# The end of an attention layer, and the start of the refinement behind a mixture of experts, arranged anew

## The reference, cut to what matters

```python
x = x + layernorm(attention(layernorm(x)))        # x: (8, 1024, 256), 16 heads of 16 + 8 dims
x = x + layernorm(ffn(layernorm(x)))

def ffn(x):                                        # 8192 rows of 256
    xf, v, integrated = x, 0, x
    idx, weight = top2(softmax(gelu(xf @ router_w1 + router_b1) @ router_w2 + router_b2))
    for _ in range(2):
        ctx = concat(integrated, v)
        shared = gelu(ctx @ shared_w1 + shared_b1) @ shared_w2 + shared_b2
        chosen = [gelu(ctx @ w1[e] + b1[e]) @ w2[e] + b2[e] for e in idx]
        # sigmoid, softplus and sigmoid of the thirds of each give a step against (x - mu);
        # the three steps are mixed, and a halting gate scales the mix
        integrated, v = ...
    refined = gelu(integrated @ refine_w1 + refine_b1) @ refine_w2 + refine_b2
    return xf + integration_weight * refined
```

## Time and profile before

| | |
|---|---|
| Median of three runs | 2930.03 us (2920.26 to 2935.52) |
| The profiled execution's own time | 2933.28 us |
| Its span | 2931.6 us |
| PE, DVE, ACT, POOL busy, share of the span | 88%, 77%, 66%, 21% |
| Mean granted TensorE clock | 0.936 of full speed |

### The profile page before, as it was taken

One profiled execution on the slowest core, in us unless ns is written; L12 is line 12 of the kernel. 1 busy time (PEld: TensorE's weight loads), 2 busy tenths in 40 slices (PEclk: granted clock), 3 DMA queues, 4 the chain that ended last, 5 costly groups with the idle time before them and its releaser, 6 DMA issues. The chain is left out here.

```text
span 2931.6 us, 43059 instructions
## 1 busy us (share of the span) xinstructions
PE 2591.9 (88%) x16032; PEld 1799.7 (61%) x16032; DVE 2269.5 (77%) x3931; ACT 1933.7 (66%) x3075; POOL 608.6 (21%) x424
## 2 busy tenths in 40 slices
PE   3788888888888967899999999999999999997997
PEld 2233333333323313688888888788788888886897
DVE  4577777667676656789889998999989988886555
ACT  1676766667676844566667666666767766665786
POOL 2012031211112111111121121211111121210476
PEclk8899989999898967899999999999999999999999
DMA  3552525254351631000000000000000000000442
GB/s 101 87 86 61 91 65 92 75 90 79 67 101 52 93 90 51 1 1 15 15 1 15 15 15 8 8 16 15 15 1 15 15 15 8 1 8 27 147 133 73
DMA packets 125634, 136.75 MB, mean 47 GB/s; under 512 B 17410, under 2 KB 105474, under 8 KB 125428
## 3 DMA queue, kind: packets, MB, share of 16 engines
q1 hardware_dynamic: 125428, 134.00, 20.1%
HBM read 87.56 MB, written 46.40 MB: 46 GB/s over the span
## 5 line engine op out<-in xcount | busy, mean ns | idle before, releaser
L491 ACT ACTIVATE probs<-psum_a 128x1024 f32<-128x1024 f32 (+3 forms) x768 | 601.1, 815 | 333.9 <-PE psum_a L807 329.6
L1487 PE MATMUL psum_f<-w,picked 128*128 128x256 f32 (+1 forms) x2304 | 712.3, 342 | 0.0
L1486 PE MATMUL psum_f<-w,picked 128*128 128x256 f32 x2304 | 617.4, 285 | 1.2 <-DVE picked L1306 1.2
L1487 PEld LDWEIGHTS psum_f<-w,picked 128*128 128x128 f32 x2304 | 444.5, 193 | 51.5
L567 DVE TENSOR_SCALAR probs<-probs 128x2048 f32<-128x2048 f32 (+3 forms) x320 | 304.0, 950 | 203.6 <-ACT probs L491 203.6
L807 PE MATMUL psum_a<-q_stack,k_stack 72*128 72x512 f16 (+3 forms) x1536 | 396.3, 349 | 56.3 <-ACT probs L491 35.0
L1486 PEld LDWEIGHTS psum_f<-w,picked 128*128 128x128 f32 x2304 | 445.1, 193 | 1.5 <-DVE picked L1306 1.5
L822 PE MATMUL psum_a<-probs,v 128*17 128x512 f32 (+3 forms) x3072 | 342.8, 520 | 10.6 <-DVE attn L579 5.9
L807 PEld LDWEIGHTS psum_a<-q_stack,k_stack 72*128 72x128 f16 x1536 | 100.6, 101 | 400.8 <-ACT probs L491 238.7
L1306 DVE TENSOR_TENSOR picked<-hid,masks 128x512 fp32r<-128x512 f32 x512 | 335.0, 714 | 10.0 <-PE psum_f L1487 6.8
L1127 ACT ACTIVATE gates<-psum_f 128x256 f32<-128x256 f32 (+1 forms) x384 | 186.4, 487 | 233.1 <-PE psum_f L1487 231.3
(11 more groups left out here) (289 smaller groups left out, 5408.2 us busy)
## 6 DMA issues: line engine op xcount, KB each, us to landing
heads_scratch<-kq_parts SPq DMA_DIRECT2D x64, 256.0 KB
k_stack<-heads_scratch SPq DMA_DIRECT2D x96, 128.0 KB
q_stack<-heads_scratch SPq DMA_DIRECT2D x96, 128.0 KB
x_in<-x_dram SPq DMA_DIRECT2D x8, 1024.0 KB, 5.5
x_res<-x_dram SPq DMA_DIRECT2D x16, 512.0 KB, 4.8
x_scratch<-y SPq DMA_DIRECT2D x16, 512.0 KB, 3.1
xs<-x_scratch SPq DMA_DIRECT2D x16, 512.0 KB, 3.9
xf_scratch<-xs SPq DMA_DIRECT2D x16, 512.0 KB, 2.9
```

The costliest lines, as they stand in the source:

```text
L491: act.activation(probs[:, s % PROB_SETS, 2 * u:2 * u + 2, q0:512], psum[:, 2 * u:2 * u + 2, q0:512], ACT.Exp, scale=exp_scale).then_inc(ex ...
L1486: pe.matmul(soft_out, x, cols[:, 1], start=start, stop=stop)
L1487: return pe.matmul(gate_out, x, cols[:, 2] if it == 0 else cols[:, 0::2], start=start, stop=stop)
```

## The change

- SP's order in window 7: the residual and the store of batch 6's first half now stand ahead of the 56 weight loads, which have moved from the end of window 6 to there. Behind them SP waits until V of batch 6 is no longer read, and loads the first 512 rows of x1 (`x_first`) over it.
- The ten split steps move from ticks 360 to 369 to ticks 373 to 382. In ticks 372 to 377 PE multiplies the unsplit weights by mu (`mean_column`, 12 matmuls), and DVE corrects the biases (job "MU").
- At tick 383 DVE takes the statistics of `x_first`, POOL the power, and at tick 386 DVE normalizes it, subtracted from mu. The mixture's PE starts with XT at once.
- The last half of batch 7 has a buffer of its own, `y_last`, so ACT's copy doesn't wait for the store. Block 1 of the mixture's rows lies over `y_last`, so its load waits until all stores have landed.
- DVE's constants (`first_values`) come behind the lower parts of block 0's transposes, not ahead of its statistics.
- Refinement's weights are loaded over the first layer's when block 15's last hidden job is done; DVE splits them in steps behind `integrate` of units 124 to 127; PE multiplies them by mu behind its last unit; the first two blocks of xf are loaded over `hid`. SP no longer waits for the last stores of xf at the end of the mixture; two loads of xf in the refinement do.

```diff
     for t, (kind, half, i) in OUTPUT.items(): ...
+    MEAN_TICK = (BATCH - 1) * STEPS + 36
+    MEAN_COLS = 6
+    job_at[MEAN_TICK + MEAN_COLS - 1] = ("MU", BATCH - 1, 0, 0)
+    SPLIT_TICK = MEAN_TICK + 1
+    X_FIRST_TICK = ALL_STEPS - 1
...
             for w in range(-1, BATCH + 1):   # SP, attention
                     load_residual(before, 0)
                     store_rows(before, 0)
                     load_residual(before, 1)
+                if w == BATCH - 1:
+                    sp.wait_ge(late_cleared, 1)
+                    for dst, src in late_loads:
+                        sp.dma_start(dst, src).then_inc(late_in, 16)
+                    sp.wait_ge(pv_done, STEPS * w)
+                    sp.dma_start(late.x_first[:], ...[0]).then_inc(x_first_in, 16)
...
-                if after == BATCH - 1:
-                    sp.wait_ge(late_cleared, 1)
-                    for dst, src in late_loads:
-                        sp.dma_start(dst, src).then_inc(late_in, 16)
...
                 if kind == "OR":
-                    if (b, half) != (0, 0):
+                    if (b, half) == (BATCH - 1, 1):
+                        act.wait_ge(pv_done, STEPS * b)
+                    elif (b, half) != (0, 0):
                         act.wait_ge(x1_stored, 16 * (2 * b + half))
-                    dst = y[:, 2 * i:2 * i + 2, :]
+                    dst = y_of(b, half)[:, 2 * i:2 * i + 2, :]
...
-                if w == BATCH - 1 and 24 <= t < 24 + late.SPLITS:
-                    split_late(t - 24)
+                if tick == X_FIRST_TICK:
+                    first_stats()
+                if tick == X_FIRST_TICK + 3:
+                    first_normalize()
+                if SPLIT_TICK <= tick < SPLIT_TICK + late.SPLITS:
+                    split_late(tick - SPLIT_TICK)
...
+            def mean_column(m):          # PE, attention
+                if m == 0:
+                    pe.wait_ge(late_in, 16 * len(late_loads))
+                    bank_free(job)
+                for c in range(2):
+                    last = pe.matmul(bank[0:w.shape[1], m:m + 1], w, late.mu_col[:, c:c + 1], ...)
...
         def _(sp):                       # mixture
-            sp.wait_ge(late.x1_stored, 16 * XS)
-            for k in range(XS):
+            for k in (2, 3, 1):
+                if k == 1:
+                    sp.wait_ge(late.x1_stored, 16 * BLOCKS)
                 sp.dma_start(xs[:, k], blk_v[k]).then_inc(x_loaded[k], 16)
-            sp.wait_ge(late.x1_stored, 16 * BLOCKS)
             for k in range(BLOCKS):
+                if k == BLOCKS - 1:
+                    job_ready(sp, ("H", k, 1, FULL - 1))
+                    for dst, src in refine_loads:
+                        sp.dma_start(dst, src).then_inc(late.f_in, 16)
+                    sp.wait_ge(upper_picked, 2 * n + 2)
+                    sp.wait_ge(lower_picked, 2 * n + 2)
+                    for q in range(2):
+                        sp.dma_start(late.xf[:, q], xf_v[q]).then_inc(late.xf_loaded[q], 16)
                 sp.wait_ge(unit_done, first_unit[k, 1] + BT)
...
-            for q in range(XS):
-                sp.wait_ge(xf_stored[q], 16 * len(range(q, BLOCKS, XS)))
...
-            x_row_stats(0)
-            first_values()
-            x_normalize(0)
             for c in range(2):
                 x_lower(0, 0, c)
+            first_values()
             x_row_stats(1)
...
+                if n >= UNITS - BT:
+                    split_refine(t)
...
-            for m in range(6):           # PE, mixture: 24 matmuls by mu, then the wait
-                ...
-            pe.wait_ge(weights_ready, 1)
...
+            pe.wait_ge(late.f_split, 2)  # PE, behind the last unit: 16 matmuls by mu
...
-            for dst, src in loads:       # SP, refinement
-                sp.dma_start(dst, src).then_inc(weights_in, 16)
             for k in range(AHEAD):
-                load_xf(k)
+                if k >= 2:
+                    load_xf(k)
                 load_x1(k)
```

More of the change, by code:

```diff
@@ L226, in attention, with y_of @@
         half_neg = sb("half_neg", [P, TILES])
+        def y_of(b, half):
+            return late.y_last if (b, half) == (BATCH - 1, 1) else y
         heads_dram = nc.dram_tensor("heads_scratch", (2, 2, 2, 2 * P, SEQ), F16, kind="Internal").ap()
@@ L1404, in _ @@
             pe.wait_ge(late.split, late.SPLITS)
-            for m in range(6):
-                for c in range(2):
-                    for part in range(2):
-                        w = w1[:, part, c, P * m:P * m + P] if m < 5 else wr1[:, part, c]
-                        last = pe.matmul(psum[0:w.shape[1], 0, m:m + 1], w.bitcast(F32), mu_col[:, c:c + 1],
-                                         start=(c == 0 and part == 0), stop=(c == 1 and part == 1))
-            last.then_inc(mu_part, 1)
-            pe.wait_ge(weights_ready, 1)
             def bank_free(job):
@@ L1517, in _, with refine @@
                     run(item)
-def refine(nc, late, x1_dram, consts_dram, w_dram, xf_dram, row_scale, out_dram):
+            for job in jobs[-3:]:
+                bank_read(pe, job)
+            pe.wait_ge(late.f_split, 2)
+            for m in range(MC):
+                for c in range(2):
+                    for part in range(2):
+                        last = pe.matmul(psum[:, 0, m:m + 1], late.wf1[:, part, c, P * m:P * m + P].bitcast(F32), mu_col[:, c:c + 1],
+                                         start=(c == 0 and part == 0), stop=(c == 1 and part == 1))
+            last.then_inc(late.f_mean, 1)
+def refine(nc, late, x1_dram, xf_dram, out_dram):
     x1_v = x1_dram.rearrange("(i t p) d -> i p t d", p=P, t=BT)
@@ L1525, in refine @@
     BLOCKS = TOKENS // BLOCK
-    mean, rstd = row_scale[:, 0], row_scale[:, 1]
+    mean, rstd = late.row_scale[:, 0], late.row_scale[:, 1]
     BUFS, AHEAD = 6, 4
@@ L1783, in _ @@
         def _(pe):
-            pe.wait_ge(weights_in, 16 * len(loads))
-            for m in range(MC):
-                for c in range(2):
-                    last = pe.matmul(psum[:, 0, m:m + 1], raw_f1[:, c, P * m:P * m + P], mu_col[:, c:c + 1], start=(c == 0), stop=(c == 1))
-            last.then_inc(mu_part, 1)
-            pe.wait_ge(weights_ready, 1)
+            pe.wait_ge(late.f_split, 4)
             for job in order:
@@ L1877 @@
         attention(nc, late, x, consts, attn_w, ffn_w, x1)
-        feed_forward(nc, late, x1, consts, ffn_w, xf, out)
+        mixture(nc, late, x1, ffn_w, xf)
+        refine(nc, late, x1, xf, out)
     r = run(nc, [arrays], core_ids=[0])
```

212 lines of the change are left out of this document (134 added, 78 removed).

## The result

The changed kernel takes 2899.39 us (median of 7 runs, 2894.30 to 2907.54) against 2930.03 (7 runs, 2920.26 to 2935.52). The ratio is 0.990, 95% interval 0.988 to 0.992: faster by 30.6 us, where 47 were forecast. 2899 lies in the range of 2868 to 2906. The places where instructions were moved gave 45.6 us in the profile, of the 46.7 that were summed for them. Part of the gain was lost again at a place where no instruction was changed: between its first and its last store the mixture took 14.2 us more. The prediction had named this as a sign of being wrong (over 3 us more or less between the mixture's first lower part and its last store): it was 1521.0 us (1183.46 to 2704.41) and is 1535.5 (1150.58 to 2686.05). So the time came out inside the range, and one step of the reasoning did not hold.

A forecast was written before the change was run, and what follows sets the result against it. The prediction took PE to bound the mixture, PE, DVE and ACT to share the attention, and PE to wait at both program borders. Its terms summed to -46.7 us, 2886.6 profiled, a median of 2883, range 2868 to 2906.

The forecast's parts named there:

- The stall: Window 7: ACT's wait for the store of `y`, behind the 56 loads, goes whole, -19.0 us; half clock behind it, -2.7.
- The rival of a moved stall: Window 7: ACT still waits for a store, or PE for late loads at tick 372; 2904 us, chance 0.10.
- The splits: Attention, window 7: leaving ticks 360 to 369 gives -13.5 us; coming to ticks 373 to 382 costs +16.3.
- cheaper splits: Ticks 373 to 382: without POOL's addition beside them the splits take 14.9 us, not 19.6; 2878 us, chance 0.12.
- The attention's end: Last clip to the mixture's start: ACT's store wait goes, less normalization and clock losses; -1.5 us, between -3.5 and +3.
- late next is the residual: Attention's end: with ACT's store wait gone, the residual's load sets the last addition; the mixture starts 3.5 us sooner.
- the rival of a cold end: Ticks 373 to 383: PE at clock 0.50 makes the stretch 41.4 us, not 36.9; end's matmuls lose 2; 2892, chance 0.13.
- The mixture's start: From the mixture program's start: XT needs only the last barrier, 0.3 us instead of 12.9; -11.6 us.
- the refinement's: Mixture's last store to refinement's XT: loads, splits and matmuls by mu move beside units 124 to 127; -15.9 us.
- The rival of an eaten gain: Mixture's first blocks: DVE-bound, unit 0 starts no sooner than 12 us after the start; -11.6 goes, 2895 us, chance 0.05.
- the change leaves its units alone, so no gain can come from there: Mixture, half of the span, PE busy 1435 of 1504 us at clock 0.97: no gain there, 0 in the sum.
- The slower rival: Mixture: a start without a pause lowers PE's granted clock, 15.5 us per hundredth; 2930 us or more, chance 0.03.

The follow-up runs named there:

- its experiment: The changed kernel with the 56 weight loads put back to the end of window 6, ahead of batch 6's first residual: 2919.42 us, ratio 0.995 against before.
- the second profile of before: The kernel before, run once more unaltered: 2931.29 us, ratio 1.000.
- the two experiments with a pause and with late refinement weights: The changed kernel with some 13 us pause ahead of the mixture, 2914.41 us; with refinement's weight loads and splits behind the mixture's last unit, 2919.42 us.
- the second pair of profiles: Both kernels run once more unaltered: the changed kernel 2900.14 us, ratio 0.989; the kernel before 2931.29 us, ratio 1.000.
- the two padded kernels: The changed kernel with the mixture's buffers from `half_neg` on, or `picked` and what lies behind it, 224 bytes further: 2892.2 us and 2891.13 us.
- its own: The kernel before with all of the mixture's buffers 288 bytes further: 2944.15 us, ratio 1.004 against before.
- six steps sooner: The changed kernel with the matmuls by mu and the ten split steps six ticks sooner: 2902.6 us, ratio 0.989 against before.

## Why the prediction was right, and where it was not

**The stall** was right in its cause, and its experiment put back 17 to 21 us. That it is right to 0.1 us in the profile is luck: with the second profile of before the same difference is 15.7 (32.4 less 16.8), and the two experiments with a pause and with late refinement weights, whose attention is the changed kernel's, had 11.6 in place of 16.8, at a clock of 1.00 and not 0.59. The rival of a moved stall fell: the store goes out 27.6 us sooner than before, and PE did not wait for the weights at step 372, thanks to the quicker issue of the loads. Behind the stall the gain was 3.6 for 2.7.

**The splits** were right in both terms, -12.5 and +16.1 for -13.5 and +16.3 (-13.3 and +13.9 in the second pair of profiles). The rival "cheaper splits" had a true core and the wrong size. The 23 split instructions sum up to 22.40 us in before and 20.37 after, and all of it is in two casts that took 3.19 us beside POOL's addition and take 1.12 alone; the first of them is the longer one. First DVE in the kernel before, then in the changed one:

```profile
1086.64 2.62 DVE L681 CAST late_up<-raw_w2z 8x768 fp32r<-8x768 f32 x1
```

```profile
1087.06 0.56 DVE L738 CAST late_up<-raw_w2z 8x768 fp32r<-8x768 f32 x1
```

The sum had 19.6 for 21.5 there, the rival 14.9. As the Trainium skill has it ("SBUF — State Buffer", "Who interferes with whom"), the two engines exclude one another, and a mask beside an addition shows it in the changed kernel too, 2.06 us and not 0.69. First POOL's addition, then the mask:

```profile
1024.72 5.39 POOL L453 TENSOR_TENSOR y<-y,x_res 128x1024 f32<-128x1024 f32 x1 [2.99 <-DVE y L712]
...
1028.60 2.06 DVE L614 SCALAR_TENSOR_TENSOR probs<-probs,tri 128x512 f32<-128x512 f32 x1 [0.70 <-ACT probs L542]
```

But in this window each addition held DVE up once, for 1.4 or 2.1 us, whatever POOL took (5.4, 5.7 or 9.0), and in windows 1 to 6 once for 1.6 or 1.7. So most of a long addition is POOL waiting: the one above ended at 1030.11, and its 2.34 of work (what an addition takes alone) reach back to 1027.8, when DVE had run out of clips. The rival let DVE lose as much as POOL, 6.6; that was wrong, and would not follow from a mutual lock either: DVE then waits for POOL's work, at most its 2.34, and not for the time that POOL waits itself. The sum's 1.2 for the two additions was less than half of what they cost DVE, 1.4 each; the second of them covers the 1.0 by which the splits' old place fell short of its 13.5.

**The attention's end** was off by 2.1: -1.5 was forecast and +0.6 came. Two parts were in the sum. What `y_last` saves was put at 3.5, and the last two additions are 7.8 us apart where they were 11.2: 3.4. But the step "late next is the residual" failed: the last addition waited for DVE, not for its load, though by an estimate not by much: issued at 1131.63, the load is there at 1136.4 by the median of 4.8 us, and the addition starts at 1136.64. So this part was right with some luck. What the end loses was put at 2.0 and came as 3.9: the first half's addition starts 15.4 us after the last clip (1128.81 less 1113.42), in before 11.5 (1146.53 less 1135.06). The normalization ahead of OT's lower parts is 1.7 of it, for 1.3 in the sum (they are done 5.4 us after the last clip, and were 3.7 after). The other 2.2, for 0.7 in the sum, came with a clock of 0.61 where it was 1.00. The rows run from the last clip to that addition, first before, then changed:

```profile
1135.06:1146.53 11.47, 9.07 (x78) 7.12 (x75) 7.46 (x23) 3.86 (x7) 1.02 (x1) 1.00 0.01 1
```

```profile
1113.42:1128.81 15.39, 11.23 (x59) 9.78 (x59) 9.86 (x28) 4.18 (x7) 2.41 (x3) 0.61 0.00 1
```

So the rival of a cold end, with a chance of 0.13, was true in one part, its 2 us for the end's matmuls, and false in the larger one: the stretch of the splits took 35.9 us and not 41.4, at a clock of 0.82 and not 0.50.

**The mixture's start** (-11.5 for -11.6) and **the refinement's** (-15.7 for -15.9) were right, and their experiments put back 12.3 and 20.6 at these places. The 20.6 is more than the term, since it puts back a longer row than before had: PE's multiplications, twice as many, behind DVE's splits and not beside them. The rival of an eaten gain fell: the mixture's first lower part comes 10.8 us after the program's start, for 22.6.

**What failed** is the step "the change leaves its units alone, so no gain can come from there", read as if no loss could: the mixture's blocks stood in the sum as 0 and came as +14.2. The instructions are unaltered, but not the addresses of their operands. The slower rival named the right engine and nearly the right size (the clock over these fifteen blocks fell from 0.979 to 0.972, and the rival had 15 us for a hundredth), but the wrong cause, a start without a pause, and it had a chance of 0.03.

By the two padded kernels some 8 to 11 us are the layout (7.7 and 8.8 by the medians of the changed kernel and its two padded ones; 11.0 for before and its own, run beside one another). The rest of the 14.2 is no larger than the scatter of the pattern of falls, 2 to 4 us from run to run. With the old residue the changed kernel is at 2891 to 2892, where the forecast was 2883. Counted against before run beside them, the two padded kernels gain 41.0 and 44.1 us of the 46.7. Of what is left, 2.1 are the attention's end, and in the first of the two 3 are in the last three blocks (221.2, for 218.0 in before), where one fall more came and one was longer; the rest is not settled, and is no larger than what the medians of before differ by from one set of runs to the next (2930.0 to 2935.2).

## What to carry to other kernels

A change that moves buffers changes code that it does not touch: compare a block of unaltered instructions at equal clock in both traces before you look for a cause among the moved ones. Where PE has a short idle time in each block, a small loss in the block's length can grow through the clock (here 0.2% at full clock became 0.9% over twelve blocks), and a pad of a few hundred bytes is a cheap thing to try: here either of two makes the changed kernel some 8 us faster by its median (10 to 14 counted against before run beside it), the best of all those run. Loads that are needed late should stand behind everything in their queue that is needed sooner, as long as they still land in time; here they did for step 372, and six steps sooner PE had to wait 2.8 us for the last of them. And take a second profile of both kernels before a term that fits to 0.1 us is believed: the stall's own length differs by 3 us between two profiles of one kernel.

## What the runs showed of the hardware

- The mean duration of the same matmuls at the same clock changed with the place of the buffers in SBUF: 282.3 ns, 280.6 or 280.7 with the mixture's buffers 288 bytes lower or 224 higher, 279.9 with only `picked` and what lies behind it 224 higher. For a program profiled twice it was the same to 0.1 ns.
- An idle time of 1.3 us, the same in each block, was followed by a fall to half clock, 0.4 to 3.3 us behind it, in 9 to 12 blocks of 12, and in the others by none. A pause of 13 us ahead changed nothing of it.
- A DVE instruction with two inputs in SBUF beside a GpSimd addition took 2.1 to 2.4 us and not 0.69, once in each addition that ran beside DVE's clips; the addition took 3.5 to 5.7 us there and 2.34 alone.
